# A layer of linear attention and routed experts: two joints, the loads and the order of an attention tile rearranged

## What is computed

```python
# attention: 16 heads of 16; sq = elu(q) + 1, and so k
out_coarse = (sq @ M) / (sq . z)                     # M, z: sums of 4 memories
outs = (sq @ fine_memories) / (sq . norms)           # each of 4
w = softmax over memories of mean over tokens (sq . norms)
out_fine = (outs * w).sum(0)
gprob = sigmoid(relu(coarse_repr @ eg_w1.T + eg_b1) @ eg_w2.T + eg_b2)
memory_output = gprob * out_fine + (1 - gprob) * out_coarse
local = causal_linear_attention(q, k, v)             # chunks of 128
output = (gate * memory_output + (1 - gate) * local) @ w_o.T
# ffn: 8 experts of width 176, the top 2 of a softmax, and a shared one of width 352
g = silu(x @ w_gate[e].T) * (x @ w_up[e].T);  y = sum_e cw[e] * (g @ w_down[e].T)
```

## Time and profile before

| | us |
|---|---|
| median of 3 runs | 674.85 (672.58 to 675.6) |
| span of the profiled execution | 683.6 |
| tokens, to the experts' first product | 0 to 221.9 |
| experts, to attention's first product | 221.9 to 384.6 |
| attention | 384.6 to 683.6 |
| busy PE, DVE, ACT, POOL | 601.4 (88%), 490.6 (72%), 342.1 (50%), 287.2 (42%) |
| moved by DMA | 88.60 MB, 130 GB/s on average |

### The profile page before, as it was taken

How to read it: one execution, slowest core, us unless ns; L and a number is a source line. 1 busy time by engine, 2 the same in 40 slices (tenths; PEclk the granted TensorE clock), 3 DMA queues, 4 the chain that set the end, 5 groups by cost and what they waited for, 6 DMA issues and landing times. The chain is left out here.

```text
span 683.6 us, 23842 instructions
## 1 busy us (share of the span) xinstructions
PE 601.4 (88%) x8665; PEld 500.9 (73%) x8665; DVE 490.6 (72%) x1461; ACT 342.1 (50%) x870; POOL 287.2 (42%) x375
## 2 busy tenths in 40 slices
PE   1999998998995999999999588988989899889995
PEld 0787786887875899999999476766766676667773
DVE  3484565465575677777777566888888888878896
ACT  4538548548544444444444334555555555555542
POOL 2055064074072830000000303567666766666664
PEclk9999999999998899999999756999999999999997
DMA  9025535446156344445554502432443244323120
GB/s 306 34 106 200 198 138 204 164 152 217 74 199 234 113 129 154 152 150 152 156 164 128 156 23 67 131 95 66 144 142 95 66 157 130 95 66 95 34 66 32
DMA packets 62230, 88.60 MB, mean 130 GB/s; under 512 B 8532, under 2 KB 48436, under 8 KB 62132
## 3 DMA queue, kind: packets, MB, share of 16 engines
q1 hardware_dynamic: 52340, 66.61, 29.3%
q0 software_dynamic: 7520, 20.07, 9.3%
q10 hardware_dynamic: 2272, 0.53, 0.4%
HBM read 46.94 MB, written 40.24 MB: 128 GB/s over the span
## 5 line engine op out<-in xcount | busy, mean ns | idle before, releaser
L1703 POOL DMA_INDIRECT yg<-d_grouped_y,from_row x64 | 63.7, 996 | 15.5 <-issue 11.6
L986 ACT ACTIVATE silu<-e_up 128x176 f32<-128x176 f32 x72 | 22.9, 318 | 91.0 <-PE e_up L91 91.0
L89 PE MATMUL e_up<-wb,xb 128*128 x144 | 51.0, 354 | 1.5 <-DVE xb L1009 1.5
L1639 DVE TENSOR_TENSOR probs<-a_ring,causal_s 128x256 f32<-128x256 f32 x128 | 45.2, 414 | 9.3 <-PE a_ring L1400 8.9
L1545 ACT ACTIVATE hid<-a_ring,b 64x128 f32<-64x128 f32 x32 | 11.6, 363 | 79.0 <-PE a_ring L1428 75.8
L1528 ACT ACTIVATE with_mem<-a_ring 128x340 f32<-128x340 f32 x128 | 46.8, 447 | 4.5 <-PE a_ring L1381 4.5
L91 PE MATMUL e_up<-wb,xb 128*128 x144 | 46.9, 326 | 0.0
L90 PE MATMUL e_up<-wb,xb 128*128 x144 | 46.8, 325 | 0.0
L833 POOL TENSOR_TENSOR ticks<-lane 128x1 f32<-128x1 f32 x4 | 2.2, 561 | 97.7 <-DVE slot_i L746 97.7
L1418 PE MATMUL a_ring<-wo,attT 128*128 128x256 f32 x128 | 37.3, 416 | 6.5 <-ACT attT L1537 3.2
L1023 DVE TENSOR_TENSOR h_sb<-e_up,silu 128x128 f32<-128x128 f32 x72 | 21.0, 292 | 29.8 <-ACT silu L986 23.0
(11 more groups left out here) (290 smaller groups left out, 2064.6 us busy)
## 6 DMA issues: line engine op xcount, KB each, us to landing
v<-d_rows SPq DMA_DIRECT2D x77, 128.0 KB, 2.0
d_grouped_y<-y_sb SPq DMA_DIRECT2D x73, 128.0 KB, 1.9
d_v<-v_half SPq DMA_DIRECT2D x8, 544.0 KB
d_q<-halves SPq DMA_DIRECT2D x8, 512.0 KB
d_k<-halves SPq DMA_DIRECT2D x8, 512.0 KB
total<-d_base SPq DMA_DIRECT2D x8, 512.0 KB
out<-total SPq DMA_DIRECT2D x7, 512.0 KB, 3.9
v<-d_v SPq DMA_DIRECT2D x6, 544.0 KB
```

What stands on the lines that cost most here:

```text
L89: pe.matmul(out, a[0], b[0], start=start, stop=False)
L1639: dve.tensor_tensor(probs[:, j, :, :], ps[:, 0:4 * CH].rearrange("p (h i) -> p h i", i=CH), causal[:, :].unsqueeze(1).broadcast_to([P, 4, ...
L1703: pool.indirect_dma_start(yg[tile % GATHERS][:, k, :], None, d["grouped_y"], bass.IndirectOffsetOnAxis(ap=c["from"][:, k, tile:tile + 1], ...
```

## The change

At the start SP issues the constant loads, the weights of the shared expert come with a semaphore for each piece, and DVE normalises batch 0. Between tokens and experts SP fetches two blocks ahead of its last store, and two more in the next phase; DVE's tables stand behind the residual of the first half; ACT's Silu table is loaded at the end of the tokens. Between experts and attention POOL, not SP, waits for the stores of y, and its first gathers are spaced between steps of the first tile; the first mask copies take 128 columns, and the rest comes behind the norms. In a tile, `gate` stands ahead of the values and the last of the four norms steps behind them. Loads and stores of attention go by tiles of 128 to 136 KB, not by halves. The core of the diff:

```diff
+            def first_rows():
+
+                for u in range(2):
+                    sp.wait_ge(s_sc[u], B // 2 * SCATTERED)
+                sp.wait_ge(s_tailed, 16 * E)
+                sp.wait_ge(s_ready, 1)
+                for j in range(2):
+                    at = sp.value_load(c["start"][0:1, j:j + 1], min_val=0, max_val=E * REGION - P)
+                    sp.dma_start(c["xg"][j], d["rows"][bass.ds(at, P), :]).then_inc(c["s_ga"][j], 16)
+
             tokens(0, s_first)
-            sp.dma_start(st_g, d["sg_t"].rearrange("(k p) n -> p k n", p=P)).then_inc(s_sw, 16)
-            sp.dma_start(st_u, d["su_t"].rearrange("(k p) n -> p k n", p=P)).then_inc(s_sw, 16)
+            sp.dma_start(st_g, d["sg_t"].rearrange("(k p) n -> p k n", p=P)).then_inc(s_sw[0], 16)
+            sp.dma_start(st_u, d["su_t"].rearrange("(k p) n -> p k n", p=P)).then_inc(s_sw[1], 16)
             sp.dma_start(st_q, d["w_qkv"]).then_inc(s_wq, 16)
             sp.dma_start(st_d[:, 0:2, :], d["sd_t"][0:2 * P, :].rearrange("(f p) n -> p f n", p=P)
-                         ).then_inc(s_sw, 16)
-            sp.dma_start(st_d[0:SF[2], 2, :], d["sd_t"][2 * P:FS, :]).then_inc(s_sw, 16)
+                         ).then_inc(s_sw[2], 16)
+            sp.dma_start(st_d[0:SF[2], 2, :], d["sd_t"][2 * P:FS, :]).then_inc(s_sw[3], 16)
+            for to, source in c["loads"][1:]:
+                sp.dma_start(to, source).then_inc(c["s_load"], 16)
             tokens(1, s_x[1])
...
                         if (s, what) == (1, "k") and b + 1 == B:
                             store_base(b, 0)
+                            first_rows()
                         store_half(b, s, what)
-            for u in range(2):
-                sp.wait_ge(s_sc[u], B // 2 * SCATTERED)
-            sp.wait_ge(s_tailed, 16 * E)
-            sp.wait_ge(s_ready, 1)
-            for j in range(UNROLL):
-                at = sp.value_load(c["start"][0:1, j:j + 1], min_val=0, max_val=E * REGION - P)
-                sp.dma_start(c["xg"][j], d["rows"][bass.ds(at, P), :]).then_inc(c["s_ga"][j], 16)
             store_base(B - 1, 1)
...
                 since(pe, s_silu, b * NB + k - 1)
+                if (b, k) == (0, 0):
+                    pe.wait_ge(s_swl, 1)
                 for kc in range(KC):
...
             act.dma_start(*c["loads"][0]).then_inc(s_ident, 16)
-            for to, source in c["loads"][1:]:
-                act.dma_start(to, source).then_inc(c["s_load"], 16)
             def shared_high(n):
                 st, parts = shared[n]
+                act.wait_ge(s_sw[n], 16)
                 act.activation(parts[0], st, ACT.Copy).then_inc(s_swh, 1)
             def normed(b, h):
-                act.wait_ge(s_rstd, b + 2 if b else h + 1)
+                act.wait_ge(s_rstd, b + 2)
                 if b == 1:
                     act.wait_ge(s_swl, 2)
                 since(act, s_sc[b % 2], SCATTERED * (b // 2))
@@ -511,12 +518,9 @@
             act.wait_ge(s_neg, 1)
             act.activation(tick_s, neg[:, 0:1], ACT.Silu)
-            normed(0, 0)
-            act.wait_ge(s_sw, 64)
             shared_high(0)
             shared_high(1)
             xT_high(0, 0)
-            normed(0, 1)
...
+            act.activation(tick_s, neg[:, 0:1], ACT.Silu)
...
+            for h in range(NS):
+                dve.wait_ge(s_rstd, h + 1)
+                for t in range(h * TS, (h + 1) * TS):
+                    dve.tensor_scalar(xn[0][:, t, :], x_in[0][:, t, :], rstd[:, t:t + 1], shift[:, t:t + 1],
+                                      ALU.mult, ALU.add).then_inc(s_xn, 1)
             shared_low(0)
+            xT_low(0, 0)
             shared_low(1)
-            xT_low(0, 0)
...
+                        table_words()
+                        token_shifts()
                 if b + 1 < B:
                     xT_low(b + 1, 0)
-                else:
-                    table_words()
-                    token_shifts()
                 residual(b, 1)
...
+            for j in range(2, UNROLL):
+                fetch(slice(j, j + 1), j)
...
-            for q in range(2):
-                sp.wait_ge(s_yst[q], 16 + 8 * SLOTS + (16 if q == 0 else 0))
...
-            act.activation(tick_s[:, :], c["lane"][:, :], ACT.Silu)
...
-            result(SLOTS + 4, 0, SLOTS * 8 + 16)
-
             dve.wait_ge(s_tables, 1)
             dve.tensor_copy(c["from"][:, :, :], c["slots"][:, :, :])
             link(dve.reciprocal(total_w, total_w))
             dve.tensor_tensor(c["cw"][:, :, :], c["cw"][:, :, :], total_w.unsqueeze(1).broadcast_to([P, TOP, NTA]),
                               ALU.mult)
+            result(SLOTS + 4, 0, SLOTS * 8 + 16)
...
-    order = [("mask", 0, 0, r) for r in range(2)] + [("norms", 0, 0, j) for j in range(NB3)]
+    order = [("mask0", 0, 0, r) for r in range(2)] + [("norms", 0, 0, j) for j in range(NB3)]
+    order += [("mask", 0, 0, r) for r in range(2)]
     tiles = [(b, t) for b in range(B) for t in range(NT)]
     for i, (b, t) in enumerate(tiles):
         order += [("scores", b, t, j) for j in range(4)]
@@ -1138,10 +1145,12 @@
         else:
             order.append(("qmean", 0, 0, 0))
         if i + 1 < len(tiles):
-            order += [("norms", *tiles[i + 1], j) for j in range(NB3)]
+            order += [("norms", *tiles[i + 1], j) for j in range(NB3 - 1)]
+        order += [("gate", b, t, 0), ("values", b, t, 0), ("values", b, t, 1)]
+        if i + 1 < len(tiles):
+            order.append(("norms", *tiles[i + 1], NB3 - 1))
         if not i:
             order += [("mean", 0, 0, 0), ("mexp", 0, 0, 0)]
-        order += [("values", b, t, 0), ("values", b, t, 1), ("gate", b, t, 0)]
...
+            def load_base(b, t):
+                n = b * NT + t
+                if b:
+                    sp.wait_ge(s_out[n % 2], 16 * ((n - NT) // 2 + 1))
+                since(sp, s_bx[n % 2], 16 * (n // 2))
+                sp.dma_start(total[:, t, :], base_src[b, :, t, :]).then_inc(s_bx[n % 2], 16)
+            def store(b, t):
+                n = b * NT + t
+                sp.wait_ge(s_sum, n + 1)
+                since(sp, s_out[n % 2], 16 * (n // 2))
+                sp.dma_start(out_v[b, :, t, :], total[:, t, :]).then_inc(s_out[n % 2], 16)
+            def load_queries(b, t):
+                tok = slice(t * P, (t + 1) * P)
+                sp.dma_start(sq_of[b % 2][:, :, tok], d["q"][b, :, :, tok]).then_inc(s_q[b % 2], 16)
+            def load_values(b, t):
+                sp.dma_start(v_of[:, b % 2, t, :, :], d["v"][b, :, t, :, :]).then_inc(s_v[b % 2], 16)
+            def load_keys(b, t):
+                tok = slice(t * P, (t + 1) * P)
+                since(sp, s_mask, (b - 1) * NS * 2 + (t // TS + 1) * 2)
+                sp.dma_start(skT[:, :, tok], d["k"][b, :, :, tok]).then_inc(s_k[t // TS], 16)
             for h in range(2):
                 of = slice(h * CH, (h + 1) * CH)
                 sp.dma_start(causal[of, :], d["causal"][of, of]).then_inc(s_causal, 16)
+            tiles = [(b, t) for b in range(B) for t in range(NT)]
+            for i, (b, t) in enumerate(tiles):
+                sp.wait_ge(ready["state"], b * STATES + 2 * t + 1)
                 if b + 1 < B:
+                    load_queries(b + 1, t)
+                if i < TS:
+                    load_base(0, 2 * t)
+                    load_base(0, 2 * t + 1)
+                sp.wait_ge(ready["values"], (b * NT + t + 1) * 2)
                 if b + 1 < B:
+                    load_values(b + 1, t)
+                    load_keys(b + 1, t)
+                if i > 1:
+                    store(*tiles[i - 2])
+                if i > 3 and tiles[i - 4][0] + 1 < B:
+                    load_base(tiles[i - 4][0] + 1, tiles[i - 4][1])
+            for b, t in tiles[-2:]:
+                store(b, t)
+            for q in range(2):
+                sp.wait_ge(s_out[q], 16 * B * NT // 2)
...
-                        since(pe, s_mask, b * NS * 2 + (t // TS + 1) * 2)
+                        if (b, t) == (0, 0):
+                            pe.wait_ge(s_mask0, 2)
+                        else:
+                            since(pe, s_mask, b * NS * 2 + (t // TS + 1) * 2)
...
+                    if what == "mask0":
+
+                        keys_there(act, 0, 0)
+                        act.activation(masked[j][:, :, 0:P], skT[:, :, 0:P], ACT.Copy,
+                                       scale=c["parity"][:, j:j + 1]).then_inc(s_mask0, 1)
+                        continue
                     if what == "mask":
                         keys_there(act, b, n)
                         since(act, ready["scores"], (b - 1) * 4 * NT + (n + 1) * 4 * TS)
-                        half = slice(n * ST, (n + 1) * ST)
+                        half = slice(n * ST + (P if (b, n) == (0, 0) else 0), (n + 1) * ST)
...
-                for tile in range(GATHERS):
-                    fetch(tile)
+                for q in range(2):
```

(55 more changed lines are left out.)

17 lines of the change are left out of this document (removed).

## The result

The changed kernel takes 692.79 us (median of 4 runs, 691.33 to 694.72), the kernel before 674.2 (4 runs, 672.58 to 675.6) beside it: a ratio of 1.0339, with a 95% interval of 1.0289 to 1.039. The direction is the forecast one, the size is not: 681.5 was forecast, and 692.79 lies above the range of 659 to 690.

The account below looks back on a forecast made before the run. It took a loop from `hid` through `yg` and POOL's gathers to bound attention's tiles. Terms -3.4 - 4.2 - 6.3 - 3 + 1.5 + 21.5 + 0.5 = +6.6 gave span 690.2, less 8.75: 681.5 us, range 659 to 690.

Parts of the forecast that it names:

- The order of the tile: Attention tiles: PE's norms wait for `hid`, `yg` comes 3.5 after it, period 9.33 for 8.47 in 25 tiles: +21.5 us.
- a loop: Attention tile: `hid` to `yg` 2.27, to POOL's second gather 4.28, to next `hid` 1.63; sum 8.18, mean period 8.47 us.
- the late signal: Attention tiles: the hidden product's signal is late while gathers are issued; `hid` starts 1.50 to 1.74 after the second gather.
- the signal comes in time: Rival, attention tiles: `hid` follows its product by 0.68, a tile takes 8.5, the order costs nothing: 660 us; chance 0.2.
- Queries at the boundaries: Batch ends in attention: norms wait for the next batch's last query slice, three times: +1.5 us, bounds 0 to 3 x 2.24.
- The start: Kernel start: VectorE normalises batch 0, first shared product at 15.2 for 18.63: -3.4 us, bounds -2.5 and -4.
- Tokens to experts: Between these phases: two fetches ahead of SP's store, first product at 217.7 for 221.90: -4.2 us, bounds -2 and -6.
- Experts to attention: Between these phases: earlier start -1.4 and earlier coarse transposition -4.9, together -6.3 us, bounds -4 and -10.
- trickling scores: Attention's first tile: the coarse transposition came behind scores that trickled from 387.23; gathers moved out of the way give -4.9 us.
- Loads by tiles: Attention's batch boundaries: big loads and stores are spread, no cost taken for smaller pieces: -3 us, bounds 0 and -5.
- Joints: Start, tokens to experts, experts to attention: gains of 3.4, 4.2 and 6.3 us in the forecast.
- The clock: Rival, start of attention and of experts: TensorE leaves its 1.2 GHz level sooner, up to -7.6 us in attention; chance 0.15.

Follow-up runs that it names:

- the second profile: The kernel before, profiled once more with no edit: span 668.0 us, its run 669.83 us.
- the old order: The changed kernel with the tile order of before, all else of the change kept: 662.95 us, ratio 0.989 to the kernel before.
- early queries: Each slice of the next batch's queries issued one tile earlier: in the changed kernel 684.78 us; with the tile order of before as well, 654.68 us.
- the best kernel: The changed kernel with the tile order of before and each slice of queries issued one tile earlier: 654.68 us, ratio 0.9793 to the kernel before.

## Why the prediction was right or wrong

**The order of the tile, forecast +21.5, measured +29.9.** The mechanism of the edit was named: the fourth norms place takes the hidden product's bank, PE takes all four at once, and so waits for `hid`; and the copy goes late. Both were confirmed, each alone, at 11.9 and 10.4. `yg` was put 3.5 after `hid`, and is 3.38 in the trace. What failed is the next step: "I read this as a loop" through POOL's gathers to the late signal. The signal's lateness was a feature of the one execution shown, and that one's mean period, 8.41, was that of the second profile, 8.43. That the lateness didn't set the period could be read from the rows of before: where `hid` came 0.69 behind its product, a tile could be as long as any other, here 501.85 - 492.97 = 8.88, and 8.56 in the third of the batches' first tiles, of which the earlier trace rows shows a short one.

```profile
492.97 0.36 ACT L1545 ACTIVATE hid<-a_ring,b 64x128 f32<-64x128 f32 x1 [2.60 <-PE a_ring L1428]
...
501.16 0.65 PE L1428 MATMUL a_ring<-coarseT,w 128*64 128x128 f32 x4
...
501.85 0.36 ACT L1545 ACTIVATE hid<-a_ring,b 64x128 f32<-64x128 f32 x1 [1.57 <-PE a_ring L1428]
```

The chain that does bind goes through VectorE's queue and the keys' bank. It was not in the forecast: that `mem_rows` reads the local product's bank, that the keys' product takes that bank next, and that everything on VectorE behind `rn` moves with it. This second link is the same in the ring of before, where the keys follow the local product seven places later too; it cost 0.7 us there, in two tiles of the old order, and 12.2 when `rn` came late. The rival "the signal comes in time" had the lateness right and still the result wrong, since its period of 8.5 was 0.56 short of this chain.

**The tile of before.** The rest of the 29.9 is in what the forecast subtracted and where it counted. It took 9.33 - 8.47 = 0.86 for 25 tiles. Measured between the old order and the changed kernel, a tile away from the batches' ends goes from 8.05 to 9.06, and the three at the ends cost nothing (34.3 in sum, then 34.5): the queries' wait covers the order there, for with early queries they go from 24.9 to 27.4. From the fifth `hid` to the last this makes 252.04 - 227.45 = 24.6, and another 4.9 fall in the four tiles ahead of that, two of which the forecast left out.

**Queries at the boundaries, forecast +1.5, measured +8.0 and +8.3.** Here the step is mis-sized. That "the hidden product and `hid` cover most of it" took the landing to be at most 2.24 and hidden; the norms started 2.63 after the issue, but a stall of PE at this place goes round the whole chain: the three tiles are longer by 2.63, 3.22 and 1.49, together 7.3.

**The start, forecast -3.4.** In place it is 15.42 for 19.11, -3.7. Alone it isn't there at the end (ratio 0.9993).

**Tokens to experts, forecast -4.2.** From the first shared to the experts' first product the changed kernel takes 193.88, the second profile of before 195.58: -1.7. SP's fetches began at 209.89 there, not at 216.83 as in the earlier trace rows; the store that held them was early enough.

**Experts to attention, forecast -6.3.** The stage's first products lie 379.31 - 374.63 = 4.68 apart, for 5.18: -0.5. The wait ahead of the first falls from 2.73 to 1.83, -0.9 where -1.4 was forecast: from the end of the last store's issue (373.29 + 0.35) to the first product it is 0.99, and the forecast put 0.5 there, a figure from no row. But from the experts' first product to attention's it is 165.33 for 164.50, so the phase as a whole didn't get shorter. The 4.9 of trickling scores was again that one execution's.

**Loads by tiles, forecast -3.** 0.9993 with the boundary's wait in it. The profiles suggest an exchange: with the loads by tiles alone the tiles at the batches' ends take 10.83, 10.94 and 12.27 and from 410.27 on none of the others is over 8.54, while the second profile of before has tiles of 12.92, 10.05 and 10.77 elsewhere. That these are stalls of the bulk loads, worth the 8 us that the early issue takes away, is argued, not tested. The Trainium skill, "DMA: Bandwidth & Descriptors", section "Measured", would have transfers of 128 KB cost more than batched ones. No such cost shows in the 0.9993, beside a DMA share of 0.33 in both kernels; what cost time was when the last piece was issued.

**The sum.** Joints and loads without the boundary's wait brought 14.7 (the best kernel against before), near the 16.9 forecast. That is luck: the joints alone bring 0.9956 in ratio, about 3 us, and the places forecast aren't those that gained. Short in the forecast are 8.4 of the order, 6.5 to 6.8 of the boundary and 2.2 of the joints and loads, about 17 us. The miss is 11.3, or 12.0 as a difference to before (+18.6 for +6.6): -14.7 + 8.3 + 29.9 = +23.5 goes by the 669.38 of before beside the experiments, and before was 674.2 beside the changed kernel, 4.8 more. The step of method that failed is the first one: a span 8.75 above the median was carried as a constant, where it said that this execution had waits that others don't have.

**The clock.** The half-clock stretch isn't gone: in the changed kernel 384 to 400 has the granted clock 0.50 with PE busy 14.98 of 16.00, and 394.60 to 419.20 has 0.81 for 0.50. That looks like the rival in part, but the second profile of before has a short stretch without the change, 0.66 from 390 to 405 and 0.98 after it:

```profile
390.00:405.00 15.00, 13.81 (x304) 11.31 (x303) 11.32 (x30) 7.32 (x21) 1.28 (x2) 0.66 0.13 37
```

So the long stretch of the earlier trace rows belongs to that execution as well, and that the change brought the clock back sooner isn't shown.

## What to carry to other kernels

Where a ring of buffers is handed out by the order of the steps, moving one step changes who waits for whom at several other steps: write down the old and the new owner of each place, and mark those that one engine takes together. Then follow the delay through the waits that stay the same, down to the first with no slack. A step that only frees one engine for a moment can close a chain through three engines and set the period of every tile. And where the profiled execution is longer than all timed runs, its extra waits must be found in a second profile before any of them is counted as a gain.

## What was not expected of the hardware

VectorE's `coarse` took 0.42 in the earlier trace rows and 0.87 in the changed kernel's tile, where POOL's sum (0.73 from 580.83) had begun before it; the order of before shows 0.42 (553.20) and 0.77 (545.29) of the same operation, the second with a sum of POOL running since 545.05. In the nine profiles of before, changed kernel and orders, leaving out each one's first two tiles, it took 0.42 or 0.43 in all 51 tiles where no sum of POOL was running at its start, and 0.42 to 0.96 where one was. TensorE stayed at its 1.2 GHz level (granted clock 0.50) for 16 us in which it was busy 94%, 384 to 400 of the changed kernel. In one execution of before `hid` started 1.0 to 2.3 us after its product's start in 23 of 28 tiles, for 0.68 or 0.69 in nearly every tile of the others, beside the same gathers; what made it so stays open.
